# GpSimd's order of work in the local attention layers: the subtraction of the row maxima between normalising q and normalising k

## The reference, cut to what matters

```python
def attn_layer(x, Wqkv, qs, ksc, Wo):      # 16 heads of 64, window 32, depth 6
    q, k, v = jnp.split(x @ Wqkv, 3, -1)
    q = l2norm(q) * qs
    k = l2norm(k) * ksc
    q = q * cos * scale + rotate_half(q) * sin * scale
    k = k * cos * inv + rotate_half(k) * sin * inv
    out = local_attention(q, k, v)
    return out @ Wo

def local_attention(q, k, v):               # each token sees its window and the one before
    sim = jnp.einsum('bhwie,bhwje->bhwij', bq, bk2) * QK_SCALE
    sim = jnp.where(mask, -jnp.finfo(sim.dtype).max, sim)
    attn = jax.nn.softmax(sim, -1)
    return jnp.einsum('bhwij,bhwje->bhwie', attn, bv2)
```

## Time and profile before

| | |
|---|---|
| median of 3 runs | 4111.85 us |
| lowest and highest | 4109.37 and 4114.33 us |
| the profiled execution | 4116.39 us, span 4113.1 us |
| granted TensorE clock over the span | 0.983 |
| busy: PE, DVE, POOL, ACT | 91%, 80%, 67%, 60% |

### The profile page before, as it was taken

How to read it: one execution, slowest core, us unless ns; L and a number is a source line. 1 busy time by engine, 2 the same in 40 slices (tenths; PEclk the granted TensorE clock), 3 DMA queues, 4 the chain that set the end, 5 groups by cost and what they waited for, 6 DMA issues and landing times. The chain is left out here.

```text
span 4113.1 us, 109635 instructions
## 1 busy us (share of the span) xinstructions
PE 3725.7 (91%) x42284; PEld 2920.0 (71%) x42284; DVE 3281.0 (80%) x4472; ACT 2477.7 (60%) x3301; POOL 2737.1 (67%) x2200
## 2 busy tenths in 40 slices
PE   5998886699999999999999999999999999999996
PEld 3776664577777777777777777777777777777774
DVE  4666664788888888888888888888888888888884
ACT  2555554466666666666666666666666666666663
POOL 2454641577676767676767677777777777777772
PEclk9999998899999999999999999999999999999998
DMA  1121111222223222232222232222322223222222
GB/s 41 57 71 71 66 64 44 58 66 65 52 67 91 70 54 63 56 96 69 59 60 59 66 93 65 59 59 61 96 67 54 64 52 103 55 71 52 64 55 62
DMA packets 157178, 267.01 MB, mean 65 GB/s; under 512 B 32062, under 2 KB 51644, under 8 KB 152380
## 3 DMA queue, kind: packets, MB, share of 16 engines
q1 hardware_dynamic: 157116, 266.19, 24.0%
HBM read 44.81 MB, written 26.21 MB: 17 GB/s over the span
## 5 line engine op out<-in xcount | busy, mean ns | idle before, releaser
L814 POOL TENSOR_TENSOR st_qk_rot<-st_qk_rot,st_qk_sq 128x1024 f32<-128x1024 f32 x384 | 920.8, 2403 | 837.3 <-DVE st_qk_sq L711 837.3
L454 PE MATMUL st_ps<-st_wqkv,st_xs 128*128 128x512 f32 x3456 | 950.6, 410 | 72.0 <-issue 36.3
L454 PEld LDWEIGHTS st_ps<-st_wqkv,st_xs 128*128 128x128 f32 x3456 | 609.1, 189 | 241.8 <-issue 96.6
L834 POOL TENSOR_TENSOR st_qk_rot<-st_qk_rot,st_rn 128x1024 f32<-128x1024 f32 x384 | 722.7, 1903 | 15.1
L562 ACT ACTIVATE st_qk_sq<-st_ps 128x1024 f32<-128x1024 f32 x384 | 393.9, 1026 | 538.4 <-PE st_ps L454 537.7
L693 DVE TENSOR_REDUCE st_nt<-st_qk_sq 128x16 f32<-128x1024 f32 x384 | 465.8, 1213 | 251.7 <-ACT st_qk_sq L562 251.6
L711 DVE TENSOR_TENSOR st_qk_sq<-st_ps,st_rot 128x512 f32<-128x512 f32 x768 | 490.3, 678 | 0.0
L697 DVE TENSOR_TENSOR st_qk_rot<-st_ps,st_rot 128x1024 f32<-128x1024 f32 x384 | 466.1, 1214 | 9.4 <-PE st_ps L469 9.4
L469 PE MATMUL st_ps<-consts_sb,st_qk_rot 128*128 128x128 f32 x3072 | 402.4, 274 | 29.8 <-DVE st_hid L794 16.8
L469 PEld LDWEIGHTS st_ps<-consts_sb,st_qk_rot 128*128 128x128 f32 x3072 | 356.0, 141 | 95.9 <-DVE st_hid L794 36.6
L462 PEld LDWEIGHTS st_ps<-st_oT,st_wo 128*128 128x128 f32 x3072 | 369.3, 192 | 68.8 <-issue 68.2
(11 more groups left out here) (141 smaller groups left out, 6636.2 us busy)
## 6 DMA issues: line engine op xcount, KB each, us to landing
st_v_bd<-st_v_tok SPq DMA_DIRECT2D x1152, 128.0 KB, 2.4
st_v_bd<-st_v_tok SPq DMA_DIRECT2D x672, 64.0 KB, 2.1
wqkv_parts<-at_w_parts SPq DMA_DIRECT2D x18, 1024.0 KB, 4.6
st_wqkv<-wqkv_parts SPq DMA_DIRECT2D x18, 1024.0 KB, 7.1
at_w_raw<-in_wqkv SPq DMA_DIRECT2D x18, 512.0 KB, 5.2
rotary_tables<-at_rot SPq DMA_DIRECT2D x6, 512.0 KB, 3.4
st_rot<-rotary_tables SPq DMA_DIRECT2D x24, 128.0 KB, 2.4
st_wo<-in_wo SPq DMA_DIRECT2D x6, 512.0 KB, 4.3
```

Source lines behind the costliest of these rows:

```text
L454: last = pe.matmul(out[:, c * 512:(c + 1) * 512], xs[:, x_part, t * P:(t + 1) * P], rhs, start=(n == 0), stop=(n == len(PASSES) - 1))
L814: pool.tensor_tensor(qk_rot[:, cols], qk_rot[:, cols], qk_sq[:, cols], ALU.add).then_inc(rot_done[a], 1)
L834: pool.tensor_tensor(view, view, rn[:, par, heads_of(a)].unsqueeze(2).to_broadcast([P, HEADS, DH]), ALU.mult).then_inc(normed[a], 1)
```

## The change

For each tile, `normalise(1)` (q is 0, k is 1) is issued behind the subtraction of the maxima instead of ahead of it. Nothing is added or removed; the semaphores and their counts are the same. In the last tiles, where there are no new q and k, and in the first tile of all, where there are no scores yet, the order stays as it was.

```diff
                             rotate(1)
                             reciprocal_norms()
                             normalise(0)
-                            normalise(1)
                         d, tt = divmod(t - 1, TILES)
                         if alive(u, d):
 
@@ -861,6 +860,8 @@
                             scores = s[:, tt % 2, :].rearrange("p (h k) -> p h k", h=HEADS)
                             pool.tensor_tensor(scores, scores, mx[:, tt % 2, :].unsqueeze(2).to_broadcast([P, HEADS, 2 * WIN]),
                                                ALU.subtract).then_inc(shifted, 1)
+                        if alive(u, 0):
+                            normalise(1)
```

## The result

| | before | after |
|---|---|---|
| median of 17 runs each | 4114.33 us | 4121.21 us |
| lowest and highest | 4109.37 and 4116.68 us | 4117.66 and 4126.02 us |
| profiled execution, its span | 4116.39 us, 4113.1 us | 4120.99 us, 4118.5 us |
| granted TensorE clock over the span | 0.983 | 0.983 |

The ratio is 1.0020 with a 95% interval of 1.0013 to 1.0028. On 4114.33 us that is 8.2 us more, 5.3 to 11.5 us. The forecast was 4114 us in a range of 4108 to 4121 us. The result lies just outside it, and the kernel became slower by about as much as a measurement can tell from no change. Of the 7.2 us between forecast and result, 2.5 us are the base: the forecast was added to a median of 3 runs, 4111.85 us, and the median of 17 runs is 4114.33 us. The rest is the change, which cost more than the 2 us forecast.

What follows compares the result with a forecast made beforehand. It took the loop of PE's q, ACT's square and DVE's long chain to set a step, PE a close second. Loop and last unit at 0 plus 2 us for the opening took 4111.85 to 4114 us, range 4108 to 4121.

Steps and rivals of the forecast that it cites:

- No gain from the earlier subtraction: POOL's subtraction comes 1.9 us earlier; its consumer L607 on ACT had 0.0 us idle before it, so gain nothing.
- Step 0: Loop unit's first step: tk late by 0.65 us, taken up by PE's idle time before ot; cost 0.
- Step 1: Loop unit's second step: k's normalising takes 2.35 us, tk 1.29 us late, absorbed before ot and h; cost 0.
- The unit: One unit of the loop stays 68.99 us long; 0.3 us or more longer would prove the reserves wrong.
- The opening: Opening units, four steps: tk 1.42 us late, partly absorbed by PE's idle times; 0.5 us a step, 2 us.
- the two idle times: Opening steps, PE: 0.61 us before ot and 0.53 us before the next q, taken as plain waits for DVE.
- The bound of 5.7 us: Opening: upper limit of its cost, if each of four steps loses the full 1.42 us delay of tk.
- The last one at 0: The last unit, behind the loop: the exchange was put at no cost there, like the loop's units.
- Rival 2: PE's added waits bring its clock down: 0.85 us for each of 92 waits, 78 us, some 4192 us; chance 0.03.
- the 92 waits of the loop: Two PE waits a unit, each priced at 0.85 us if the clock fell: 78 us.
- Rivals 1 and 4: 1: idle before ot is no wait, 4148 us, chance 0.07; 4: nothing shows at all, 4112 us, chance 0.12.
- Rival 3: The exponential does wait somewhere, so the earlier subtraction helps: at most 87 us, 4025 us; chance 0.03.

Runs made afterwards that it cites:

- e2_loop: The exchange only in the loop over units 2 to 46, the kernel before elsewhere; 4113.29 against 4111.73 us, ratio 1.0004.
- e4_early_round: The changed kernel with ACT's rounding L547 ahead of the copy of k in units 0 and 1; 4115.95 against 4111.73 us, ratio 1.0013.
- e5_odd: The exchange only in odd steps of units 0 and 1, the kernel before elsewhere; 4115.69 us in one run, kernel before 4111.46 us.
- e6_even: The exchange only in even steps of units 0 and 1, the kernel before elsewhere; 4110.79 us in one run, kernel before 4111.46 us.
- e3_last: The exchange only in the last unit with a q and k (47), the kernel before elsewhere; 4113.69 against 4111.73 us, ratio 1.0006.
- e8_no_floor_exchanged: The changed kernel without DVE's L704; ACT adds the floor as bias of its logarithm, POOL reads plain sums; 4069.99 against 4116.36 us, ratio 0.9892.
- e9_late_round: The kernel before, no exchange, with ACT's rounding L547 one place later, behind L617, in units 0 and 1; 4117.86 against 4111.46 us, ratio 1.0013.

## Why the prediction was right in the loop and wrong in the sum

- **No gain from the earlier subtraction.** Right. L607 has 0.0 us of idle time before it, as in the earlier trace rows.
- **Step 0.** Right in kind: tk's loads wait 0.66 us for the 0.65 forecast, and step 0 is not longer. The idle time before ot fell to 0.42 us and not to 0.2. Once they have waited, tk's eight loads take 0.85 us and not 1.03 us, as the rows of both kernels show, so they make up 0.18 us.
- **Step 1.** Right: k's L834 took the 2.35 us, tk's wait was 1.28 us for the 1.29 forecast, the idle time before ot vanished, and that before h is 1.18 us for the 1.3 forecast.
- **The unit.** 69.04 us, against the limit of 0.3 us above 68.99 which I had set. The 0.042 us a unit, 1.9 us in all, were forecast as zero. Step 1 is the one that is longer, 20.963 us in the mean for 20.921, and 20.954 and 20.952 us in e2_loop and e4_early_round; kernels with the old order in the loop have 20.920 to 20.923, and e5_odd 20.943. Kernels with the old order in the loop range from 68.991 to 69.011 us a unit, with e5_odd at 69.030, and those with the new one from 69.026 to 69.043. The difference is barely larger than this spread. Most of it enters at DVE's L704 in step 1, which takes 1.11 us in the mean over the units in place of 1.08, beside POOL; DVE's instructions behind it are 0.03 us late. Why it takes longer stays open.
- **The opening: the step that failed.** "Since the two idle times are plain waits for DVE, I take ... 0.5 us a step, 2 us." It measured 4.6 us. I put the part that the two idle times of PE don't take at 0.5 us a step, because I followed the delay of tk only along PE, to its next two waits for DVE. For that path the size was not bad: e6_even and e4_early_round leave 1.1 us of it. The delay goes along ACT as well. ACT takes k from PE, and further down its queue, behind the copies of k and of v and the exponential, stands the rounding, which had 0.68 us in hand before its consumer on DVE fell behind a POOL instruction. The bound of 5.7 us did hold the 4.6 us, but by luck: it was worked out from delays of tk on PE.
- **"The last one at 0": the other step that failed.** It measured 2.8 us, 3.5 us in e3_last and 2.4 us in e4_early_round and e8_no_floor_exchanged. The argument for the loop was that v and ot give reserves behind a late tk. Behind the last unit there is no k or v, and I had not read a single row there. The wait of 0.80 us that already stood there, with POOL named as its releaser, says that no reserve is left.
- **Rival 2, the clock.** Wrong for the 92 waits of the loop: the unit's granted clock is still 1.00. Right at the last unit's tk, whose wait of 2.66 us is the longest that the change made: 0.88 us. The row of 3.66 us behind which the transposes took 1.88 us, 0.85 us more than at full clock, was the right price for it in this execution and in e3_last; in others it was less.
- **Rivals 1 and 4** are out: step 0's delay did not run through, and there is something to see. Rival 3, a gain from the earlier subtraction, is out by the row of L607.
- **Slips in the working.** The loop has 45 units (2 to 46) and not 46; no term of the sum hangs on that, as the loop was put at 0. By the rule given, the range is 4109.5 to 4120.2 us; it was written 1.5 and 0.8 us wider.

With 4.6 us for the opening, 1.9 for the loop and 2.8 for the end the sum would have been 9.3 us, within the 5.3 to 11.5 us measured.

A row of the trace of before would have told the opening's part. In unit 0 the same collision is already there, POOL first by 0.53 us (POOL, DVE):

```profile
774.24 2.35 POOL L814 TENSOR_TENSOR st_qk_rot<-st_qk_rot,st_qk_sq 128x1024 f32<-128x1024 f32 x1 [2.06 <-DVE st_qk_sq L711]
774.77 2.11 DVE L667 TENSOR_TENSOR st_xs<-xT_sb,st_xs 128x256 fp32r<-128x256 f32 x1 [0.60 <-ACT st_xs L547]
```

A line whose instructions take 0.41 us in most places and 2.11 us in one is a sign that its length hangs on a neighbour; the next question is how near that neighbour is in the other places.

## What to carry to other kernels

Follow a delay along every engine that takes the late result, to the end of that engine's queue in the step, and look there for instructions that could start behind an operation of another engine beside which they were seen to stand still: which of two comes first can be worth more than the delay itself. The reserve is the time between the moment when the input is ready and the moment when it is used, and not the distance to the neighbour. Reserves found in the loop hold for the loop; read the first and the last units by themselves, and treat a wait that already names the delayed producer as no reserve at all. When a change is worth less than the scatter of whole runs, exchange one place at a time and compare stretches between the same two instructions.

## What the runs showed of the hardware

**A DVE operation with two inputs in SBUF, L667, stood still for a POOL operation that began before it.** It (128x256) took 0.41 us when it started 0.16 us ahead of POOL's L814, and 2.58 us, 2.56, 2.29, 2.21, 2.16 and 2.11 us when it started 0.06, 0.08, 0.35, 0.43, 0.48 and 0.53 us behind it: the later it came, the less it had left to wait, and it ended 0.28 or 0.29 us behind POOL's end each time. L732, which reads one input from PSUM, took 1.21 us beside L814 in the kernel before, and the same 1.21 us when L814 had ended in the kernel after. The one that was first paid little: L814 took 2.35 to 2.36 us with DVE behind it, and 2.48 us when DVE was ahead. This goes beyond the mean: a change of 0.24 us in the order of starts (0.16 ahead to 0.08 behind) changed DVE's time by 2.15 us. The Trainium skill says in "SBUF — State Buffer", section "Who interferes with whom": "Issue order, not op shape, decides who blocks." These rows agree: the same DVE instruction took 0.41 us when it was first and up to 2.58 us when it was second.

**Behind a wait of 2.65 us PE ran more slowly, but it didn't begin at once each time.** Behind a wait of 1.10 us (the kernel after, opening) the eight transposes took 1.06 us, as they do behind the 0.80 us in the kernel before. Behind 2.65 or 2.66 us at the end, tk, ot and sim took 1.94, 1.74 and 1.95 us in the kernel after, 1.94, 1.92 and 2.76 us in e3_last, 1.60, 1.91 and 1.95 us in e4_early_round, and 1.16, 1.91 and 2.37 us in e8_no_floor_exchanged, for 1.06, 1.04 and 1.95 us in the kernel before. The row of the last one's tk:

```profile
3984.03 1.16 PE L473 MATMUL st_ps<-consts_sb,st_qk_rot 128*128 128x128 f32 x8 [2.65 <-POOL st_qk_rot L834]
```

So a short first job doesn't mean that the clock was kept; the job behind it was slow in each of the four. Of the 2.4 to 3.5 us that the end cost in these four, the POOL instruction has 1.9 us, and the slower jobs the other 0.5 to 1.7 us, most in e3_last. Behind PE's 2.96 us of idle time in e9_late_round six projections took 2.86 instead of 1.66 us. What sets the moment and the extent was not tested.
